# A two-layer sequence block in 32 chunks: the last chunk's mixer products inside the feed-forward part ahead of it, and its result added by VectorE

## The chip, the cores and the metric

The kernel runs on one core of one Trainium2 chip. A core has TensorE (PE) for matrix products, VectorE (DVE), ScalarE (ACT) and GpSimd (POOL) for element-wise work, and SyncE (SP), whose queue issues DMAs. Each runs its instructions in order and they wait for each other by semaphores. The metric is the device time of one execution in microseconds.

## What is computed

Input `x` is 16 x 1024 x 256 (float32). The reference, cut to what matters:

```python
x = x + attn(layernorm(x))     # called the mixer here
x = x + ffn(layernorm(x))

# attn(x)
phi = cumsum((x @ W_omega.T + b_omega) * exp(log_scale) / sqrt(position))
cm_real, cm_imag = x * cos(phi), x * sin(phi)
mem_real = cumsum(cm_real) / position; mem_imag = cumsum(cm_imag) / position
ret_real = mem_real * cos(phi) + mem_imag * sin(phi)
ret_imag = mem_imag * cos(phi) - mem_real * sin(phi)
h = layernorm(concat(cm_real, cm_imag, ret_real, ret_imag)) * gamma + beta
attn = x + gelu(h @ W1.T + b1) @ W2.T + b2      # 1024 -> 512 -> 256

# ffn(x), W1 and W2 rounded to -1, 0, 1
ffn = relu(x @ Wq1.T + b1) @ Wq2.T + b2         # 256 -> 1024 -> 256
```

## The kernel before

The 16384 rows are cut into 32 chunks of 512 (`CHUNKS`, numbered 0 to 31). Float32 operands are split in a high and a low float16 part, so most products come twice or three times. The code of each engine is written out by hand as a loop over steps (`run`, `step`); in step s four to five chunks are in work at once: `now` is chunk s in its feed-forward part, `nxt` (s+1) in the mixer's hidden layer, gelu and output product, `ahead` (s+2) and `far` (s+3) in the phases, scans and first layernorm. The order of the calls in each engine's `step` is the order of its instructions. Near the end of the program `far`, then `ahead`, then `nxt` no longer exist: step 30 has chunk 30 as `now` and chunk 31 as `nxt`, step 31 has chunk 31 alone.

What TensorE does in a step: `hidden(nxt, 0..3)` (L914, 4 x 24 products of 512 columns) with the statistics and `spread` between them; then eight blocks `ffn_in(now, m)` (L929, 4 products of 512 columns each) and `ffn_out(now, m)` (L942, 8 products of 256 columns each), block m out being three blocks (`LAG`) behind block m in; ahead of the last three blocks out comes `mixer_out(nxt, now)` (L959, 48 products of 256 columns).

PSUM, `ps`, has eight banks of 512 float32. Banks 0 and 1 (`ps_rows_a`) take `ffn_out`, banks 4 to 7 `hidden` and then, by turns, the eight blocks of `ffn_in`. `mixer_out` writes banks 4 and 5 (`ps_rows_b`), so it waits until ScalarE has read blocks 4 and 5 of `now` (`relu_done`). Bank 2 holds `spread` (read by ScalarE, L656, `rbs_done`) and bank 3 the sums of the context (read by VectorE, `csq_done`); banks 2 and 3 hold `omega` of `far` where that exists.

Per block of the feed-forward part ScalarE makes `relu` (L694) and its float16 high part `relu_hi` (L703), VectorE the low part `relu_lo` (L1309), in four slots (`SLOTS`); `ffn_out` needs both parts. For the mixer VectorE scales the hidden sums (`scale_hidden`, L1265), ScalarE makes `gelu` (L660) and `gelu_hi` (L666), VectorE `gelu_lo` (L1270).

Behind `mixer_out` a chunk goes through a chain: VectorE adds the residual (`mixer_residual`, L1277, into `x1`), takes the statistics (L1284, L1289, L1295), GpSimd raises to the power -1/2 (L495), VectorE makes the mean term (`lean_2`, L1101), ScalarE normalises (`normalise_2`, L595, four pieces) and makes the high part (`second_hi`, L676), VectorE the low part (`second_lo`, L1301), and SyncE issues four DMA transposes into `turned2` (L440), which `ffn_in` of the chunk reads. These transposes also wait until all blocks `ffn_in` of the chunk before are done (`f1_done`).

The output: GpSimd adds the bias `f_b2` to `x1` by an accumulating DMA (`x1_bias`, L487), SyncE stores `x1` (L452), ScalarE overwrites `x1` with the scaled sums of `ffn_out` (`output`, L608), and GpSimd adds that to what is stored by an accumulating DMA (`output_sum`, L491). GpSimd's queue has, in a step, `inverse_std_2(now)`, `output_sum(before)`, then `x1_bias(now)`.

## Time and profile before

| | |
|---|---|
| median of 3 runs | 1565.07 us (1564.71 to 1565.65) |
| the profiled execution | 1566.02 us |
| its span, first to last instruction | 1564.2 us |
| TensorE busy | 1481.0 us (95%) |
| VectorE, ScalarE, GpSimd busy | 1393.2, 1251.6, 585.8 us |
| mean granted clock of TensorE | 0.985 of full speed |

The span is one execution as the hardware profiler took it; the time of the execution has 1.8 us more around it. TensorE works nearly without a break from about 100 us to 1524 us; a step takes about 43 us in the later part. The page gives busy time as an average over the whole span, so the first and last stages don't show in it, and the timelines of the last 85 us are read for them. A line of a timeline is: start, time, engine, line of the kernel, operation, what it writes and reads, count, and in brackets how long the engine stood before it and who released it.

### The profile page before, as it was taken

The numbers are of one execution on the slowest core, as the hardware profiler recorded it, in microseconds if no ns is written. First come the engines' busy times: TensorE is split into PE (matmuls) and PEld (weight loads), VectorE is DVE, ScalarE is ACT, GpSimd is POOL, SyncE is SP. The second block draws the span as 40 slices with busy tenths as digits, with TensorE's granted clock in tenths as the row PEclk, the third lists the DMA queues.
The fourth block names the chain that finished last, engine by engine and source line by source line (L and its number), as shares of the span: only waits on it lengthen the run. The fifth ranks groups of instructions, "written<-read, shape, count | busy, mean of one in ns | idle before, by whom it ended". The sixth has DMA issues, their size and how long they took to land.

```text
span 1564.2 us, 29917 instructions
## 1 busy us (share of the span) xinstructions
PE 1481.0 (95%) x10677; PEld 875.1 (56%) x10677; DVE 1393.2 (89%) x2322; ACT 1251.6 (80%) x1774; POOL 585.8 (37%) x395
## 2 busy tenths in 40 slices
PE   3789999999999999999999999999999999999994
PEld 2455555665555566555556555555556555655652
DVE  6999999999999999999999999999999999998831
ACT  6768987888888888888878888888788988888743
POOL 1323344443334444333444433344433344433311
PEclk9799999999999999999999999999999999999997
DMA  6325665545665554566555457655555665545424
GB/s 215 70 53 109 122 112 85 107 96 93 118 122 104 93 105 95 95 118 122 99 95 105 95 96 121 122 90 99 101 96 104 122 120 83 105 87 93 82 55 67
DMA packets 234115, 159.25 MB, mean 102 GB/s; under 512 B 140784, under 2 KB 224240, under 8 KB 233968
## 3 DMA queue, kind: packets, MB, share of 16 engines
q0 software_dynamic: 59904, 83.90, 34.9%
q1 hardware_dynamic: 172432, 69.77, 19.2%
q10 hardware_dynamic: 1632, 3.67, 0.6%
q8 instruction: 86, 1.41, 0.4%
q14 instruction: 61, 0.50, 0.1%
HBM read 24.13 MB, written 33.55 MB: 37 GB/s over the span
## 4 chain that ended last, share of the span: by engine, by line
PE 45%; DVE 30%; issue 11%; ACT 6%; SPq 4%; DMA 3%; DVEq 0%; ACTq 0%; POOL 0%; POOLq 0%
PE ps L942 11%; PE ps L959 10%; PE ps L914 10%; PE ps L929 8%; PE ps L874 5%; SPq L440 4%; DVE ph L1152 3%; DVE mi L1184 2%; DMA turned<-rows 2%; DVE mr L1196 2%; DVE bn L1284 2%; DVE mi L1215 2%; DVE xs L1129 2%; DVE rows L1301 2%; DVE arena L1265 2%
## 5 line engine op out<-in xcount | busy, mean ns | idle before, releaser
L914 PE MATMUL ps<-arena,w_hi 128*128 128x512 f16 x2048 | 609.0, 379 | 2.1 <-DVE arena L1241 1.2
L914 PE MATMUL ps<-arena,w_lo 128*128 128x512 f16 x1024 | 388.0, 379 | 0.0
L914 PEld LDWEIGHTS ps<-arena,w_hi 128*128 128x128 f16 x2048 | 197.9, 98 | 223.4 <-issue 2.0
L929 PE MATMUL ps<-turned,fw_t 128*128 128x512 f16 x1024 | 250.1, 382 | 22.6 <-DMA turned<-rows 22.1
L942 PE MATMUL ps<-fw_t,arena 128*128 128x256 f16 x2048 | 254.7, 272 | 9.9 <-DVE arena L1309 9.0
L942 PEld LDWEIGHTS ps<-fw_t,arena 128*128 128x128 f16 x2048 | 193.7, 97 | 92.8 <-issue 39.0
L694 ACT ACTIVATE arena<-ps,relu_bias,relu_scale 128x512 f32<-128x512 f32 x256 | 191.7, 773 | 55.3 <-PE ps L929 55.2
L527 POOL TENSOR_TENSOR sqr<-sqr,turn 128x1024 f32<-128x1024 f32 x32 | 88.8, 2776 | 334.1 <-ACT sqr L642 320.5
L1309 DVE TENSOR_TENSOR arena<-arena 128x512 f16<-128x512 f32 x256 | 170.1, 685 | 28.3 <-ACT arena L703 27.6
L959 PE MATMUL ps<-w_hi,arena 128*128 128x256 f16 x1024 | 173.0, 273 | 0.0
L929 PEld LDWEIGHTS ps<-turned,fw_t 128*128 128x128 f16 x1024 | 98.6, 98 | 124.5 <-DMA turned<-rows 35.8
L914 PEld LDWEIGHTS ps<-arena,w_lo 128*128 128x128 f16 x1024 | 100.1, 98 | 120.8
L703 ACT CAST arena<-arena 128x512 f16<-128x512 f32 x256 | 148.0, 616 | 1.0
L959 PE MATMUL ps<-w_lo,arena 128*128 128x256 f16 x512 | 139.6, 273 | 0.0
L543 POOL TENSOR_TENSOR qa<-mi,sn 128x1024 f32<-128x1024 f32 x32 | 76.6, 2393 | 96.5 <-DVE mr L1196 86.7
L959 PEld LDWEIGHTS ps<-w_hi,arena 128*128 128x128 f16 x1024 | 100.2, 98 | 11.6
L660 ACT ACTIVATE arena<-arena,b_full,z_down 128x512 f32<-128x512 f32 x128 | 100.5, 809 | 1.2 <-DVE arena L1265 0.8
L495 POOL TENSOR_TENSOR rs<-ve,minus_half 128x4 f32<-128x4 f32 x32 | 59.4, 1856 | 97.9 <-DVE ve L1295 97.1
L1270 DVE SCALAR_TENSOR_TENSOR arena<-arena,up 128x512 f16<-128x512 f32 x128 | 94.8, 743 | 0.0
L646 ACT CAST sqr<-sqr 128x512 f16<-128x512 f32 x32 | 19.8, 618 | 91.8 <-POOL sqr L529 91.8
L476 POOL DMA_DIRECT2D rr<-qa x32 | 29.8, 932 | 169.1 <-DVE rr L1231 169.1
L666 ACT ACTIVATE arena<-arena,up 128x512 f16<-128x512 f32 x128 | 90.8, 710 | 0.0
(183 smaller groups left out, 2774.8 us busy)
## 6 DMA issues: line engine op xcount, KB each, us to landing
x_rows<-in_L_attn_x SPq DMA_DIRECT2D x32, 512.0 KB, 4.3
rr<-qa POOLq DMA_DIRECT2D x32, 512.0 KB, 5.0
ri<-qb POOLq DMA_DIRECT2D x32, 512.0 KB, 7.0
base<-bias_rows POOLq DMA_DIRECT2D x32, 512.0 KB, 6.1
x<-bias_rows POOLq DMA_DIRECT2D x32, 512.0 KB, 8.7
out<-x SPq DMA_DIRECT2D x32, 512.0 KB, 5.5
out<-x POOLq DMA_DIRECT2D x32, 512.0 KB, 6.1
arena<-in_L_attn_W ACTq DMA_DIRECT2D x1, 2048.0 KB, 11.3
```

The costliest lines, as they stand in the source:

```text
L527: pool.tensor_tensor(sqr[:, :, :], sqr[:, :, :], turn[:, :, :], ALU.add).then_inc(q2_done, 1)
L660: act.activation(z[:, m], z[:, m], ACT.Gelu, scale=z_down[:, 0:1], bias=b1_full[:, m:m + 1])\
L666: act.activation(gh[:, m], z[:, m], ACT.Copy, scale=up[:, 3:4]).then_inc(gh_done[m], 1)
L694: act.activation(rf[:, m % SLOTS], ps[:, 4 + m % KE], ACT.Relu, scale=relu_scale[:, 0:1], bias=relu_bias[:, m:m + 1]).then_inc(relu_done, 1)
L703: act.copy(rh[:, m % SLOTS], rf[:, m % SLOTS]).then_inc(rh_done, 1)
L874: last = pe.matmul(ps[:, 2 + e], w[:, k, e * P:(e + 1) * P], a[:, k], start=(i == 0), stop=(i == len(passes) - 1))
L914: last = pe.matmul(ps[:, 4 + m], w[:, k, m * P:(m + 1) * P], a[:, c.b, k], start=(i == 0), stop=(i == len(passes) - 1))
L929: last = pe.matmul(ps[:, 4 + m % KE], fw1_t[:, k, m * P:(m + 1) * P], a[:, k], start=(i == 0), stop=(i == len(passes) - 1))
L942: last = pe.matmul(ps_rows_a[:, j], a[:, m % SLOTS, j * P:(j + 1) * P], fw2_t[:, m], start=(m == 0 and j % 2 == 0 and a is rh), stop=(m == ...
L959: last = pe.matmul(ps_rows_b[:, j], a[:, m, j * P:(j + 1) * P], w[:, m], start=(i == 0), stop=(i == len(passes) - 1))
L1270: dve.scalar_tensor_tensor(out=gl[:, m], in0=z[:, m], scalar=up[:, 3:4], in1=gh[:, m], op0=ALU.mult, op1=ALU.subtract).then_inc(gl_done[m], 1)
L1309: dve.tensor_tensor(rl[:, m % SLOTS], rf[:, m % SLOTS], rh[:, m % SLOTS], ALU.subtract)\
```

## The change

It touches steps 30 and 31 of each engine.

- TensorE: `mixer_out` of chunk 31 comes right behind the first four blocks `ffn_in` of chunk 30, ahead of the first block `ffn_out`, and writes banks 2 and 3 (`ps_rows_last`); it waits for `rbs_done` and `csq_done` and no longer for blocks 4 and 5 of relu. The first four blocks `ffn_in` of chunk 31 get a wait for the relu of chunk 30's blocks 4 to 7.
- ScalarE: in step 30 (`last_mixer`) all of chunk 31's gelu comes ahead of chunk 30's relu, each `relu_hi` stands right behind its `relu`, and `normalise_2` and `second_hi` of chunk 31 stand ahead of relu 6. In step 31 `output(30)` is followed by the relus by pairs; the last `output` is gone.
- VectorE: in step 30 `second_lo(30)` comes ahead of `context_variance(31)`, the four `gelu_lo` in a row, and residual and statistics of chunk 31 ahead of relu_lo 3, `lean_2` ahead of relu_lo 5, `second_lo` ahead of relu_lo 6. At the end it has a new `output`, two instructions that add the scaled sums to `x1`.
- SyncE stores chunk 31 in two halves, each behind its add, and not before; GpSimd's last accumulating store is gone.

The order of instructions as built shows it. TensorE, from the first blocks of chunk 30's feed-forward part on, before (`fw_t` with `turned` is ffn_in, `fw_t` with `arena` is ffn_out, `w_hi` and `w_lo` with 128x256 are the mixer's output weights):

```order
L929 MATMUL ps<-turned,fw_t 128x512 x16
L942 MATMUL ps<-fw_t,arena 128x256 x8
L929 MATMUL ps<-turned,fw_t 128x512 x4
L942 MATMUL ps<-fw_t,arena 128x256 x8
...
L942 MATMUL ps<-fw_t,arena 128x256 x8
L959 MATMUL ps<-w_hi,arena 128x256
L959 MATMUL ps<-w_lo,arena 128x256
...
L959 MATMUL ps<-w_hi,arena 128x256
L942 MATMUL ps<-fw_t,arena 128x256 x24
L929 MATMUL ps<-turned,fw_t 128x512 x16
L942 MATMUL ps<-fw_t,arena 128x256 x8
```

and after:

```order
L965 MATMUL ps<-turned,fw_t 128x512 x16
L999 MATMUL ps<-w_hi,arena 128x256
L999 MATMUL ps<-w_lo,arena 128x256
...
L999 MATMUL ps<-w_hi,arena 128x256
L978 MATMUL ps<-fw_t,arena 128x256 x8
L965 MATMUL ps<-turned,fw_t 128x512 x4
L978 MATMUL ps<-fw_t,arena 128x256 x8
L965 MATMUL ps<-turned,fw_t 128x512 x4
...
L978 MATMUL ps<-fw_t,arena 128x256 x32
L965 MATMUL ps<-turned,fw_t 128x512 x16
L978 MATMUL ps<-fw_t,arena 128x256 x8
```

The 48 products stood behind five blocks out and eight in; now they stand behind four blocks in, and all eight blocks out come after them.

ScalarE, from relu 4 of chunk 30 on (L694, L700: relu; L703, L709: relu_hi; `xs`: normalise_2; `rows`: second_hi; `x<-ps`: output), before:

```order
L694 ACTIVATE arena<-ps,relu_bias,relu_scale 128x512 x2
L703 CAST arena<-arena 128x512 x2
L694 ACTIVATE arena<-ps,relu_bias,relu_scale 128x512 x2
L703 CAST arena<-arena 128x512 x2
L608 ACTIVATE x<-ps,down 128x1024
L595 ACTIVATE xs<-x,lean,rs 128x256 x4
L676 CAST rows<-xs 128x4x256
L694 ACTIVATE arena<-ps,relu_bias,relu_scale 128x512
L703 CAST arena<-arena 128x512
```

and after:

```order
L700 ACTIVATE arena<-ps,relu_bias,relu_scale 128x512
L709 CAST arena<-arena 128x512
L700 ACTIVATE arena<-ps,relu_bias,relu_scale 128x512
L709 CAST arena<-arena 128x512
L601 ACTIVATE xs<-x,lean,rs 128x256 x4
L682 CAST rows<-xs 128x4x256
L700 ACTIVATE arena<-ps,relu_bias,relu_scale 128x512
L709 CAST arena<-arena 128x512
L700 ACTIVATE arena<-ps,relu_bias,relu_scale 128x512
L709 CAST arena<-arena 128x512
L614 ACTIVATE x<-ps,down 128x1024
L700 ACTIVATE arena<-ps,relu_bias,relu_scale 128x512
```

Chunk 31's normalisation stood behind all relus of chunk 30 and its output; now it stands between blocks 5 and 6.

VectorE, from the first relu_lo of chunk 30 on (L1309, L1359: relu_lo; L1270: gelu_lo), before:

```order
L1309 TENSOR_TENSOR arena<-arena 128x512 x3
L1270 SCALAR_TENSOR_TENSOR arena<-arena,up 128x512 x2
L1309 TENSOR_TENSOR arena<-arena 128x512
...
L1270 SCALAR_TENSOR_TENSOR arena<-arena,up 128x512
L1309 TENSOR_TENSOR arena<-arena 128x512 x3
L1277 SCALAR_TENSOR_TENSOR x<-ps,h_down,base 128x1024
L1284 BN_STATS bn<-x 128x6 x4
...
L1295 TENSOR_SCALAR ve<-mv 128x4
L1101 SCALAR_TENSOR_TENSOR lean<-rs,mv 128x4
L1301 TENSOR_TENSOR rows<-xs,rows 128x4x256
```

and after:

```order
L1320 SCALAR_TENSOR_TENSOR arena<-arena,up 128x512 x4
L1359 TENSOR_TENSOR arena<-arena 128x512 x3
L1327 SCALAR_TENSOR_TENSOR x<-ps,h_down,base 128x1024
L1334 BN_STATS bn<-x 128x6 x4
...
L1345 TENSOR_SCALAR ve<-mv 128x4
L1359 TENSOR_TENSOR arena<-arena 128x512 x2
L1151 SCALAR_TENSOR_TENSOR lean<-rs,mv 128x4
L1359 TENSOR_TENSOR arena<-arena 128x512
L1351 TENSOR_TENSOR rows<-xs,rows 128x4x256
L1359 TENSOR_TENSOR arena<-arena 128x512 x10
L1367 SCALAR_TENSOR_TENSOR x<-ps,down,x 128x512 x2
```

Residual, statistics and mean term moved ahead of five, then three of the low parts, and two adds stand at the end.

The diff:

```diff
@@ line 203 of before @@
         ps_rows_b = ps[:, 4:6, :].rearrange("p b (t d) -> p (b t) d", d=D)
+        ps_rows_last = ps[:, 2:4, :].rearrange("p b (t d) -> p (b t) d", d=D)
 
@@ line 449 of before @@
                                      rows1[:, j].rearrange("p i d -> p (i d)"), transpose=True).then_inc(turned1_done, 16)
-                if c := s.chunk(0):
+                if (c := s.chunk(0)) and c.index < CHUNKS - 1:
                     need_dma(sp, x1_biased, c)
@@ line 454 of before @@
             run(sp, step, -2)
-            for i in range(2):
-                sp.wait_ge(stored[i], 16 * (CHUNKS // 2))
-                sp.wait_ge(added[i], 16 * (CHUNKS // 2))
+            last = Chunk(Counts(sp, CHUNKS - 2), 1)
+            for half in range(2):
+                need(sp, out_done, last, 0 if half == 0 else -1)
+                sp.dma_start(out_v[last.index][:, 2 * half:2 * half + 2],
+                             x1[:, last.b, 2 * half:2 * half + 2]).then_inc(stored[last.b], 16)
+            sp.wait_ge(stored[0], 16 * (CHUNKS // 2))
+            sp.wait_ge(added[0], 16 * (CHUNKS // 2))
+            sp.wait_ge(stored[1], 16 * (CHUNKS // 2 + 1))
+            sp.wait_ge(added[1], 16 * (CHUNKS // 2 - 1))
 
@@ line 558 of before @@
             run(pool, step, -1)
-            output_sum(Chunk(Counts(pool, CHUNKS - 2), 1))
 
@@ line 704 of before @@
 
+            def last_mixer(before, now, last):
+
+                sums_hi(last)
+                output(before)
+                normalise_2(now)
+                second_hi(now)
+                spread_out(last)
+                for m in range(KE - 1):
+                    gelu(last, m)
+                for m in range(KE - 1):
+                    gelu_hi(last, m)
+                gelu(last, KE - 1)
+                gelu_hi(last, KE - 1)
+                for m in range(KF):
+                    if m == KF - 2:
+                        normalise_2(last)
+                        second_hi(last)
+                    relu(now, m)
+                    relu_hi(now, m)
+
             def step(s):
                 before, now, nxt, ahead, far = s.chunk(-1), s.chunk(0), s.chunk(1), s.chunk(2), s.chunk(3)
+                if now and not ahead:
+                    if nxt:
+                        last_mixer(before, now, nxt)
+                    else:
+                        output(before)
+                        for m in range(KF):
+                            relu(now, m)
+                            relu_hi(now, m)
+                    return
                 if nxt:
@@ line 849 of before @@
             run(act, step, -1)
-            output(Chunk(Counts(act, CHUNKS - 2), 1))
 
@@ line 926 of before @@
                     need(pe, z_done[m], after)
+                else:
+                    need_block(pe, relu_done, m + KE, c, 1)
                 passes = [(a, k) for k in range(KD) for a in (h2, l2)]
@@ line 947 of before @@
             def mixer_out(c, before):
-                if before:
+                if before and c.index < CHUNKS - 1:
                     need_block(pe, relu_done, KE, before)
@@ line 955 of before @@
                     need(pe, gl_done[m], c)
+                if c.index == CHUNKS - 1:
+                    need(pe, rbs_done, c)
+                    need(pe, csq_done, c)
+                rows = ps_rows_last if c.index == CHUNKS - 1 else ps_rows_b
                 for j in range(NT):
@@ line 958 of before @@
                     for i, (a, w, m) in enumerate(passes):
-                        last = pe.matmul(ps_rows_b[:, j], a[:, m, j * P:(j + 1) * P], w[:, m],
+                        last = pe.matmul(rows[:, j], a[:, m, j * P:(j + 1) * P], w[:, m],
                                          start=(i == 0), stop=(i == len(passes) - 1))
@@ line 978 of before @@
                     hidden(nxt, 3)
+                if now and not ahead:
+                    for m in range(KF):
+                        ffn_in(now, m, nxt)
+                        if nxt and m == KE - 1:
+                            mixer_out(nxt, now)
+                        if m >= LAG:
+                            ffn_out(now, m - LAG)
+                    for m in range(KF - LAG, KF):
+                        ffn_out(now, m)
+                    return
                 for m in range(KF):
@@ line 1276 of before @@
                 need_dma(dve, added, c, 2)
-                dve.scalar_tensor_tensor(out=x1[:, c.b], in0=ps_rows_b, scalar=h_down[:, 0:1], in1=base[:, c.b],
-                                         op0=ALU.mult, op1=ALU.add).then_inc(x1_done, 1)
+                dve.scalar_tensor_tensor(out=x1[:, c.b], in0=ps_rows_last if c.index == CHUNKS - 1 else ps_rows_b,
+                                         scalar=h_down[:, 0:1], in1=base[:, c.b], op0=ALU.mult, op1=ALU.add).then_inc(x1_done, 1)
 
@@ line 1311 of before @@
 
+            def output(c):
+                need_block(dve, f2_done, KF - 1, c)
+                need_dma(dve, x1_biased, c)
+                for half in range(2):
+                    to = x1[:, c.b, 2 * half:2 * half + 2]
+                    dve.scalar_tensor_tensor(out=to, in0=ps_rows_a[:, 2 * half:2 * half + 2], scalar=down[:, 4:5],
+                                             in1=to, op0=ALU.mult, op1=ALU.add).then_inc(out_done, 1)
+
+            def last_mixer(now, last):
+
+                lean_2(now)
+                second_lo(now)
+                context_variance(last)
+                for m in range(KE):
+                    scale_hidden(last, m)
+                for m in range(KE):
+                    gelu_lo(last, m)
+                for m in range(KF):
+                    if m == 3:
+                        mixer_residual(last)
+                        statistics_2(last)
+                        spread_2(last)
+                    if m == 5:
+                        lean_2(last)
+                    if m == 6:
+                        second_lo(last)
+                    relu_lo(now, m)
+
             def step(s):
                 now, nxt, ahead, far = s.chunk(0), s.chunk(1), s.chunk(2), s.chunk(3)
+                if now and not ahead:
+                    if nxt:
+                        last_mixer(now, nxt)
+                    else:
+                        for m in range(KF):
+                            relu_lo(now, m)
+                        output(now)
+                    return
                 if now:
```

## Rows read from the trace of the kernel before

**Rows 1.** The page: the span, and three of its groups of instructions (count, busy us, mean ns)

```profile
span 1564.2 us, 29917 instructions
...
L694 ACT ACTIVATE arena<-ps,relu_bias,relu_scale 128x512 f32<-128x512 f32 x256 | 191.7, 773 | 55.3 <-PE ps L929 55.2
...
L1309 DVE TENSOR_TENSOR arena<-arena 128x512 f16<-128x512 f32 x256 | 170.1, 685 | 28.3 <-ACT arena L703 27.6
...
L703 ACT CAST arena<-arena 128x512 f16<-128x512 f32 x256 | 148.0, 616 | 1.0
...
```

**Rows 2.** Busy us (and instructions) by stage, then granted clock, DMA share, GB/s

```profile
...
1524.00:1538.00 14.00, 0.00 (x0) 0.00 (x0) 2.02 (x8) 4.21 (x6) 3.60 (x3) 0.59 0.72 113
1538.00:1544.00 6.00, 5.74 (x15) 2.11 (x16) 0.69 (x1) 2.58 (x4) 0.00 (x0) 0.53 0.25 87
...
1556.00:1564.00 8.00, 0.00 (x0) 0.00 (x0) 0.00 (x0) 0.72 (x1) 1.29 (x1) 0.79 0.51 66
...
```

**Rows 3.** Timeline of TensorE: start us, us, instruction, idle before and releaser

```profile
...
1504.16 3.62 PE L929 MATMUL ps<-turned,fw_t 128*128 128x512 f16 x16
1507.99 1.03 PE L942 MATMUL ps<-fw_t,arena 128*128 128x256 f16 x8 [0.21 <-DVE arena L1309]
...
1515.92 0.27 PE L959 MATMUL ps<-w_hi,arena 128*128 128x256 f16 x1
...
1521.05 0.27 PE L959 MATMUL ps<-w_hi,arena 128*128 128x256 f16 x1
1521.16 2.78 PE L942 MATMUL ps<-fw_t,arena 128*128 128x256 f16 x24
1538.26 6.27 PE L929 MATMUL ps<-turned,fw_t 128*128 128x512 f16 x16 [14.31 <-DMA turned<-rows]
...
1553.67 1.91 PE L942 MATMUL ps<-fw_t,arena 128*128 128x256 f16 x16 [0.45 <-DVE arena L1309]
```

**Rows 4.** Timeline of VectorE, columns as before

```profile
...
1504.36 0.69 DVE L1265 TENSOR_TENSOR arena<-ps,rb 128x512 f32<-128x512 f32 x1 [2.62 <-PE ps L914]
...
1521.36 1.28 DVE L1277 SCALAR_TENSOR_TENSOR x<-ps,h_down,base 128x1024 f32<-128x1024 f32 x1 [3.50 <-PE ps L959]
...
1525.90 0.16 DVE L1101 SCALAR_TENSOR_TENSOR lean<-rs,mv 128x4 f32<-128x4 f32 x1 [1.13 <-POOL rs L495]
1529.36 1.23 DVE L1301 TENSOR_TENSOR rows<-xs,rows 128x1024 f16<-128x1024 f32 x1 [3.30 <-ACT rows L676]
...
```

**Rows 5.** Timeline of ScalarE

```profile
...
1526.18 2.07 ACT L595 ACTIVATE xs<-x,lean,rs 128x256 f32<-128x256 f32 x4 [1.08 <-DVE lean L1101]
...
1555.61 1.11 ACT L608 ACTIVATE x<-ps,down 128x1024 f32<-128x1024 f32 x1 [2.30 <-PE ps L942]
```

**Rows 6.** Timeline of SyncE's queue

```profile
...
1495.52 5.12 SPq L440 DMA_TRANSPOSE turned<-rows  x4
...
1530.67 6.32 SPq L440 DMA_TRANSPOSE turned<-rows  x4
...
```

**Rows 7.** Timeline of GpSimd

```profile
...
1557.02 1.29 POOL L491 DMA_DIRECT2D out<-x  x1 [27.17 <-ACT x L608]
```

**Rows 8.** DMA issues, 1494 to 1510 us, then 1556 on: KB, us to landing

```profile
...
out<-x SPq DMA_DIRECT2D x1, 512.0 KB, 3.1
turned<-rows SPq DMA_TRANSPOSE x4, 2.5
...
out<-x POOLq DMA_DIRECT2D x1, 512.0 KB, 6.1
```

**Rows 9.** Stages as in rows 2, short ones in which the granted clock changed

```profile
...
92.00:94.00 2.00, 0.00 (x0) 0.00 (x0) 2.00 (x3) 1.97 (x4) 0.00 (x0) 0.74 0.44 90
1526.50:1527.00 0.50, 0.00 (x0) 0.00 (x0) 0.00 (x0) 0.50 (x2) 0.50 (x1) 0.58 0.00 0
1543.50:1544.00 0.50, 0.50 (x4) 0.17 (x3) 0.00 (x0) 0.40 (x1) 0.00 (x0) 0.86 0.00 0
...
```

**Rows 10.** Timeline of TensorE, early in the program

```profile
...
94.04 0.26 PE L1023 MATMUL ps<-rows,x 128*128 128x128 f16 x1 [3.10 <-ACT fw_t L784]
...
```

## The prediction

> **What bounds the kernel now.** I read the page first, then the busy time by stage, then the timeline of each engine behind 1500 us. The span is 1564.2 us [rows 1] and the profiled execution took 1566.02 us; the three timed runs have their median at 1565.07 us. So 1.8 us lie outside the span, and the profiled execution is 0.95 us above the median. The diff leaves all of the program up to chunk 29's feed-forward part as it was, so the sum is made over the last 85 us of the span and the difference is taken off both numbers.
>
> In that tail TensorE sets the pace up to 1523.9 us and then the kernel is a chain of latencies. TensorE does nothing between 1524 and 1538 us [rows 2]: its timeline shows chunk 30's feed-forward products, then chunk 31's mixer products (L959, 1515.92 to 1521.32), 24 products left over from chunk 30, and 14.31 us of waiting for the DMA transposes of chunk 31 [rows 3]. What it waits for can be followed step by step. VectorE adds the residual at 1521.36, takes the statistics, GpSimd the power, VectorE has the mean term at 1525.90 [rows 4], ScalarE normalises at 1526.18 [rows 5], VectorE's low part runs 1529.36 to 1530.59 [rows 4], SyncE issues four transposes from 1530.67 on [rows 6], and the products start at 1538.26. Behind the last product (1555.58) come ScalarE's copy at 1555.61 [rows 5], GpSimd's accumulating store at 1557.02 [rows 7], and the end at 1564.2. Nothing else is running in either wait, so a microsecond taken out of these two chains is a microsecond of the kernel.
>
> **The mixer products of chunk 31 come 8 us earlier.** TensorE's order of instructions in chunk 30's part becomes: four blocks in (L929's 16 products), mixer_out of chunk 31 (48 products), and then the eight blocks out and four blocks in by turns. The products are the same in number; they write banks 2 and 3 in place of 4 and 5. Those are free once ScalarE has copied the spread and VectorE has read the sums, long before, so the two added waits (rbs_done, csq_done) cost nothing. When can they start? TensorE has the 16 products done at 1504.16 + 16 x 0.216 = 1507.6. Every low part of the gelu must be there: VectorE's fourth scale_hidden starts at 1504.36 and takes 0.69 [rows 4]; in the new order ScalarE does gelu 3 and gelu_hi 3 right behind it, ahead of all of relu, and VectorE has four gelu_lo in a row. By 0.77 + 0.62 us on ScalarE and about 0.7 us on VectorE (L694, L703 and L1309 are of the same size of tile) [rows 1] that is 1505.05 + 0.77 + 0.62 + 0.69 = 1507.2 for the fourth low part behind its high part, or, counted along VectorE's four in a row, 1505.05 + 4 x 0.69 = 1507.8. Before, TensorE also stood 0.21 us here for the first relu_lo, until 1507.99 [rows 3]. So I put the mixer products at 1507.95, their end at 1507.95 + 5.40 = 1513.35 and the residual at 1513.4 instead of 1521.36.
>
> From there the chain is the same as before, with two things in its way. VectorE has relu_lo 3 and 4 between the statistics and the mean term: the power is there at 1513.4 + 4.5 = 1517.9, and the two pieces, 0.65 us each, run from 1516.8 to 1518.1, so 0.2 us is lost. ScalarE has relu 5 and its high part ahead of the normalisation; block 5 is in at 1513.2 + 4 x 0.87 = 1516.7, and 0.77 + 0.62 us later it is 1518.1, so nothing is lost. The normalisation thus starts at 1518.4, not 1526.18: **7.8 us earlier**. Behind it ScalarE's order holds relu 6 and 7 back until 1521.4 and TensorE stands some 2 us in chunk 30's last three blocks and ends them near 1525.9 instead of 1523.9. That is off the path: the transposes need only all eight blocks in (1520.1), and chunk 30's result is out of the banks (ScalarE, 1.1 us) by 1527.0, before chunk 31 needs them. POOL's bias for chunk 31 now stands behind the accumulating store of chunk 30 and so goes out at 1528, 0.3 us earlier than before at best; it is needed only near 1543.
>
> **The transposes.** SyncE took 6.32 us to issue the four of chunk 31 and 5.12 for those of chunk 30 [rows 6], and the last lands 2.5 us behind its issue [rows 8]. In the slow case GpSimd's store of chunk 30 and its bias for chunk 31 were moving in the same 4 us. Now the transposes go out from 1522.9 to 1528.0 and that store, which waits for 1527, can have no byte moving before that, when the last of the four (1526.8) is already out. I take 5.12, **1.2 us less**. Issue of the fourth at 1522.9 + 3.85, landing 2.5, and TensorE starts at 1529.25: 9.0 us earlier than 1538.26. Its wait shrinks from 14.3 to some 3.35 us.
>
> **The clock.** Before, the granted clock fell to its lower level (1.2 of 2.4 GHz) at 1526.6, 2.7 us behind the last product, and came back at 1543.6, 5.4 us after the products had begun again [rows 9]; half of these 5.4 us, 2.7, is lost. A wait of 3.10 us early in the trace [rows 10] also had a fall in it, 2.0 us behind the last product [rows 9]. So a wait of 3.35 us with some 2 us of standing just ahead of it very probably has one too, and what is saved is small. The loss has 0 (no fall) and about 3 us as its ends; I take 2.2, a little under the 2.7 of the nearest row because the engine has been idle for less, so **0.5 us less**. The Trainium skill's page "TensorE: Matmul & The Clock Gate" (Part 1 and the section on oscillation behind it) says that the throttled state is the default and that activity releases it, and names waits for DMA in a loop as what throttles it again; this trace agrees, with the falls at 1526.6 us and before 94 us, both in idle stretches [rows 9]. By that rule alone the shortening of the wait would return nothing at all here, and the forecast would be 0.5 us higher.
>
> **The last feed-forward part.** 32 products in and 64 out take the same 13.9 us at the full clock. ScalarE now has each high part right behind its relu, so the stand of 0.45 us before the last 16 products [rows 3] goes: 1.39 us per block of ScalarE [rows 1] against 1.73 us of TensorE keeps up. **0.5 us less.**
>
> **The last result.** Before: from the last product at 1555.58 to 1564.2, 8.6 us: copy 1.1, GpSimd's issue at 1557.02, landing 6.1 us later [rows 7, 8], 1.1 us of closing. Now: VectorE adds two halves straight from the banks. One half has the size of a scale_hidden (0.69), the whole that of the residual (1.28) [rows 4], so both are done at +1.35; SyncE issues each half behind it, and the plain store of a whole chunk landed 3.1 us after its issue in a quiet stretch [rows 8]. A half has half the bytes: between 1.55 and 3.1, I take 2.5, since part of 3.1 is not data. 0.05 + 1.35 + 0.1 + 2.5 + 1.1 = 5.1, so **3.5 us less**. The bias of chunk 31 has landed long before and costs nothing; if it had not, this add is what would wait. "DMA: Bandwidth & Descriptors" of the Trainium skill (the sections Specifications and Latency and other measured facts) gives 0.6 us against 1 us as the latency to the first byte of a store from SyncE and from GpSimd. By that alone the path would save 0.4 us on the queue; the rows show 3.1 against 6.1 us for the same 512 KB, and the rows decide.
>
> **Sum.** 7.8 + 1.2 + 0.5 + 0.5 + 3.5 = 13.5 us. 1564.2 becomes 1550.7 in the span, the profiled execution 1552.5, and the median 1565.07 - 13.5 = 1551.6 us, 0.9% less.
>
> **Rivals.**
> (a) The clock does not fall in the shorter wait. For it: it fell 2.0 and 2.7 us behind a last product, so its moment is not fixed. Against: both are under 3.35. It would give 2.2 us more, 1549.4.
> (b) The store or the transposes are slow: the transposes again take 6.32 us, or ScalarE's and VectorE's new interleaving holds the normalisation back by a relu pair (1.4 us), or the halves need 3.1 us each to land. Each is 0.6 to 1.4 us and they can add up: 1553 to 1554.5.
> (c) The change does not do what it says, the mixer products find gelu_lo late and TensorE stands with chunk 30's blocks queued behind them. Each microsecond of that is one on the path. With the mixer products starting where they did, at 1515.92 [rows 3], only the tail's 3.5 and 0.5 would be left: 1561. Against it: the order shows gelu 3 and its parts ahead of the relus.
> (d) Slower than before: the stand of 0.3 us ahead of the mixer products and the later ones let the clock fall within chunk 30 and it stays low. Then 5.4 us of mixer products take 5.4 more and the last part 13.9 - 2.2 more: 13.5 is outweighed by 17.1, 1568.7. It decides from 13.5 us of extra work at the lower level on the path. Against it: the stand of 0.21 us at 1507.99 left the clock at its full level, and it came back in 5.4 us the one time it was low here.
>
> **How the numbers follow.** Forecast 0.72, (a) 0.10, (b) 0.14, (c) 0.02, (d) 0.01, and 0.01 for a gain within the bound. The forecast's own ends are the loss to the clock at 1.2 to 2.9 us and the landing at 1.6 to 3.1: 1549.7 to 1552.9. The range takes in (a) and (b): 1548.9 to 1554.4. A measurement of this kernel can tell 0.2%, 3.1 us, from no change. All of the forecast, (a), (b) and (c) is faster by more than that: 0.98; same 0.01, slower 0.01.
>
> **What would show it.** TensorE's timeline: mixer products from 1508, first products of chunk 31 at 1529.2, a wait of 3 to 3.5 us before them, with the clock falling in or just ahead of it. SyncE: transposes from 1522.9, 5.1 us long. VectorE: residual at 1513.4 and the normalisation on ScalarE at 1518.4. At the end two adds of 0.7 us and the end of the span some 5.1 us after the last product. I am wrong if the residual starts after 1515, if TensorE's stand inside chunk 30 reaches the eight blocks in (then the transposes wait for them), or if the stores land after more than 3.1 us.

## The result, and the profile after

| | before | after |
|---|---|---|
| median | 1565.14 us (6 runs, 1562.27 to 1565.88) | 1551.21 us (6 runs, 1549.32 to 1552.36) |
| profiled execution, its span | 1566.02, 1564.2 us | 1552.36, 1550.6 us |
| mean granted clock | 0.985 | 0.990 |

The ratio is 0.9912, with a 95% interval of 0.9899 to 0.9925: 13.9 us less. The forecast was 1551.6.

TensorE's timeline of the changed kernel answers to [rows 3] (L965 is ffn_in, L978 ffn_out, L999 mixer_out):

```profile
1504.34 3.62 PE L965 MATMUL ps<-turned,fw_t 128*128 128x512 f16 x16
1508.24 0.27 PE L999 MATMUL ps<-w_hi,arena 128*128 128x256 f16 x1 [0.28 <-issue]
...
1513.48 1.04 PE L978 MATMUL ps<-fw_t,arena 128*128 128x256 f16 x8
...
1524.23 1.03 PE L978 MATMUL ps<-fw_t,arena 128*128 128x256 f16 x8 [1.90 <-DVE arena L1359]
1525.56 1.03 PE L978 MATMUL ps<-fw_t,arena 128*128 128x256 f16 x8 [0.30 <-DVE arena L1359]
1530.54 5.31 PE L965 MATMUL ps<-turned,fw_t 128*128 128x512 f16 x16 [3.95 <-DMA turned<-rows]
...
1542.64 3.66 PE L978 MATMUL ps<-fw_t,arena 128*128 128x256 f16 x32
```

The 48 mixer products start at 1508.24 behind a stand of 0.28 us and end when block 0 out begins, 1513.5; before it was 1515.92 to 1521.3. The wait before the last part is 3.95 us and not 14.31, and the last 32 products run without a stand. VectorE's rows, to be held against [rows 4], and GpSimd's power:

```profile
1513.68 1.28 DVE L1327 SCALAR_TENSOR_TENSOR x<-ps,h_down,base 128x1024 f32<-128x1024 f32 x1 [2.14 <-PE ps L999]
...
1518.60 0.16 DVE L1151 SCALAR_TENSOR_TENSOR lean<-rs,mv 128x4 f32<-128x4 f32 x1 [0.30 <-POOL rs L502]
...
1522.06 1.23 DVE L1351 TENSOR_TENSOR rows<-xs,rows 128x1024 f16<-128x1024 f32 x1 [2.70 <-ACT rows L682]
...
1546.33 1.41 DVE L1367 SCALAR_TENSOR_TENSOR x<-ps,down,x 128x512 f32<-128x512 f32 x2 [1.34 <-PE ps L978]
```

```profile
1517.17 1.39 POOL L502 TENSOR_TENSOR rs<-ve,minus_half 128x4 f32<-128x4 f32 x1 [21.56 <-DVE ve L1345]
```

ScalarE's normalisation ([rows 5] has it at 1526.18) and SyncE's queue ([rows 6]); in the last row the two stores of the halves:

```profile
1518.88 2.08 ACT L601 ACTIVATE xs<-x,lean,rs 128x256 f32<-128x256 f32 x4 [0.30 <-DVE lean L1151]
```

```profile
1488.71 7.34 SPq L441 DMA_TRANSPOSE turned<-rows  x4
...
1523.37 5.74 SPq L441 DMA_TRANSPOSE turned<-rows  x4
1547.11 1.03 SPq L459 DMA_DIRECT2D out<-x  x2
```

DMA issues of the changed kernel, first in the stretch of the transposes (1523 to 1531 us), then behind 1538 us, to be held against [rows 8]. In the upper part stand also the queues (packets and MB behind the title, share of the 16 engines):

```profile
DMA packets 2212, 0.58 MB, mean 73 GB/s; under 512 B 2176, under 2 KB 2210, under 8 KB 2210
...
q14 instruction: 1, 0.01, 1.1%
q8 instruction: 1, 0.02, 0.8%
...
out<-x POOLq DMA_DIRECT2D x1, 512.0 KB, 6.4
...
turned<-rows SPq DMA_TRANSPOSE x4, 2.9
```

```profile
out<-x SPq DMA_DIRECT2D x2, 256.0 KB, 2.2
```

The spans differ by 1564.2 - 1550.6 = 13.6 us. To see where they went I count from TensorE's first product of chunk 30's part, because the program's way up to there isn't equally long in two executions (below). It starts at 1504.16 before and 1504.34 after; from there to the end it is 60.0 us before and 46.3 after:

| piece | before | after | difference | forecast |
|---|---|---|---|---|
| chunk 30's part begins, to the first transpose's issue | 26.51 | 19.03 | 7.5 | 7.8 |
| first transpose's issue, to the last part's first product | 7.59 | 7.17 | 0.4 | 1.2 |
| last part: lost to the lower clock | 2.7 | 1.7 | 1.0 | 0.5 |
| last part: the rest | 14.6 | 14.05 | 0.6 | 0.5 |
| last product, to the end of the span | 8.63 | 4.31 | 4.3 | 3.5 |

The sum was right to 0.3 us, but two of its terms were off by 0.8: what the transposes did not give, the clock and the last store did. That the errors cancel is luck, and the closeness of the sum says less than the terms do. Differences here and below are taken before rounding. The experiments below take the terms one by one.

### The profile page after: what moved, and what is told of

The parts are those of the page before. It is cut to its first block, busy times and chain, and to the rows that moved or that the text cites. A ratio compares the mean times of both kernels' runs of the same rounds, so it can differ in the third digit from the quotient of the medians.

```text
span 1550.6 us, 29919 instructions
## 1 busy us (share of the span) xinstructions
PE 1480.5 (95%) x10677; PEld 875.2 (56%) x10677; DVE 1395.3 (90%) x2324; ACT 1252.0 (81%) x1773; POOL 583.3 (38%) x394
## 3 DMA queue, kind: packets, MB, share of 16 engines
q8 instruction: 86, 1.41, 0.4%
## 4 chain that ended last, share of the span: by engine, by line
PE 47%; DVE 30%; issue 9%; ACT 5%; SPq 4%; DMA 4%; DVEq 0%; ACTq 0%; POOL 0%; POOLq 0%
PE ps L978 11%; PE ps L948 11%; PE ps L999 10%; PE ps L965 8%; PE ps L908 5%; SPq L441 4%; DVE ph L1202 3%; DVE mi L1234 3%; DMA turned<-rows 2%; DVE mr L1246 2%; DVE bn L1334 2%; DVE xs L1179 2%; DVE mi L1265 2%; DVE rows L1351 2%; DVE arena L1315 2%
## 5 line engine op out<-in xcount | busy, mean ns | idle before, releaser
L978 PE MATMUL ps<-fw_t,arena 128*128 128x256 f16 x2048 | 254.6, 272 | 11.9 <-DVE arena L1359 10.9
L965 PE MATMUL ps<-turned,fw_t 128*128 128x512 f16 x1024 | 249.1, 381 | 11.5 <-DMA turned<-rows 11.1
L978 PEld LDWEIGHTS ps<-fw_t,arena 128*128 128x128 f16 x2048 | 193.7, 97 | 94.0 <-issue 39.3
L700 ACT ACTIVATE arena<-ps,relu_bias,relu_scale 128x512 f32<-128x512 f32 x256 | 191.8, 773 | 49.0 <-PE ps L965 49.0
L1359 DVE TENSOR_TENSOR arena<-arena 128x512 f16<-128x512 f32 x256 | 170.6, 686 | 20.6 <-ACT arena L709 19.8
L999 PE MATMUL ps<-w_hi,arena 128*128 128x256 f16 x1024 | 173.2, 273 | 0.3 <-issue 0.3
L965 PEld LDWEIGHTS ps<-turned,fw_t 128*128 128x128 f16 x1024 | 98.3, 98 | 112.7 <-DMA turned<-rows 25.0
L709 ACT CAST arena<-arena 128x512 f16<-128x512 f32 x256 | 148.6, 616 | 1.5
L999 PE MATMUL ps<-w_lo,arena 128*128 128x256 f16 x512 | 139.7, 273 | 0.0
L999 PEld LDWEIGHTS ps<-w_hi,arena 128*128 128x128 f16 x1024 | 100.3, 98 | 12.4 <-issue 0.7
L1315 DVE TENSOR_TENSOR arena<-ps,rb 128x512 f32<-128x512 f32 x128 | 82.1, 683 | 10.9 <-ACT rb L662 6.5
```

Source lines behind the costliest of these rows:

```text
L700: act.activation(rf[:, m % SLOTS], ps[:, 4 + m % KE], ACT.Relu, scale=relu_scale[:, 0:1], bias=relu_bias[:, m:m + 1]).then_inc(relu_done, 1)
L709: act.copy(rh[:, m % SLOTS], rf[:, m % SLOTS]).then_inc(rh_done, 1)
L965: last = pe.matmul(ps[:, 4 + m % KE], fw1_t[:, k, m * P:(m + 1) * P], a[:, k], start=(i == 0), stop=(i == len(passes) - 1))
L978: last = pe.matmul(ps_rows_a[:, j], a[:, m % SLOTS, j * P:(j + 1) * P], fw2_t[:, m], start=(m == 0 and j % 2 == 0 and a is rh), stop=(m == ...
L999: last = pe.matmul(rows[:, j], a[:, m, j * P:(j + 1) * P], w[:, m], start=(i == 0), stop=(i == len(passes) - 1))
L1315: dve.tensor_tensor(z[:, m], ps[:, 4 + m], rb[:, :], ALU.mult).then_inc(z_done[m], 1)
```

## How the runs are compared

The table gives, for the one profiled execution of each kernel, the pieces that the timelines show, in us. "To first product" is from the issue of the first transpose of chunk 31 to TensorE's first product with it; in e3 part of it is TensorE itself, which was still busy with added products. "Clock" is half of the time in the last part at the lower level. "From chunk 30" is from chunk 30's first product in to the end of the span. Median and ratio are those of the runs of that label.

| kernel | chunk 30 begins | to first product | last part | clock | last product to end | from chunk 30 | median | ratio (95%) |
|---|---|---|---|---|---|---|---|---|
| before | 1504.16 | 7.59 | 17.32 | 2.7 | 8.63 | 60.0 | 1565.14 | |
| changed | 1504.34 | 7.17 | 15.75 | 1.7 | 4.31 | 46.3 | 1551.21 | 0.9912 (0.9899 to 0.9925) |
| e1 | 1504.03 | 7.44 | 16.52 | 2.5 | 8.39 | 51.4 | 1556.78 | 0.9957 (0.9942 to 0.9972) |
| e2 | 1500.19 | 7.57 | 17.18 | 2.6 | 4.25 | 55.5 | 1558.13 | 0.9964 (0.9950 to 0.9977) |
| e3 | 1503.31 | 7.98 | 14.06 | 0 | 4.24 | 45.3 | 1550.33 | 0.9913 (0.9900 to 0.9927) |
| e4 | 1502.64 | 7.66 | 15.75 | 1.7 | 4.83 | 47.3 | 1551.66 | 0.9920 (0.9908 to 0.9933) |
| e5 | 1500.86 | 9.13 | 16.97 | 3.0 | 4.27 | 54.5 | 1556.45 | 0.9954 (0.9941 to 0.9967) |
| e6 | 1503.90 | 7.25 | 16.67 | 2.7 | 4.25 | 47.2 | 1553.59 | 0.9935 (0.9920 to 0.9950) |
| e7 | 1500.58 | 9.46 | 16.72 | 2.1 | 4.22 | 49.4 | 1551.69 | 0.9927 (0.9914 to 0.9940) |
| e8 | 1503.34 | 8.04 | 14.07 | 0 | 4.23 | 45.4 | 1549.66 | 0.9915 (0.9898 to 0.9931) |
| e9 | 1502.15 | 6.88 | 16.70 | 2.7 | 4.24 | 46.9 | 1550.49 | 0.9920 (0.9905 to 0.9935) |
| e10 | 1501.92 | 6.38 | 15.73 | 1.7 | 4.24 | 45.4 | 1550.47 | 0.9926 (0.9909 to 0.9942) |
| e11 | 1501.40 | 6.38 | 15.75 | 1.7 | 4.29 | 45.6 | 1549.31 | 0.9914 (0.9900 to 0.9929) |
| e12 | 1502.97 | 6.39 | 14.07 | 0 | 4.25 | 43.7 | 1548.58 | 0.9912 (0.9898 to 0.9925) |

The second column is the warning in this table: up to there TensorE has the same work (e9 to e12 have 64 products of one column more at the head), and it takes from 1500.2 to 1504.3 us. So a median carries some 2 us that have nothing to do with the edit, and the kernel before itself had medians of 1564.32, 1563.50, 1562.48 and 1563.23 us beside the experiments. Effects of 1 us are read from the column "from chunk 30" and from the rows.

## Experiments: the two halves of the change

**e1: the last result as before.** On the changed kernel:

```diff
 # SyncE: stores chunk 31 before the sum again, in one piece; its two stores at the end go
-                if (c := s.chunk(0)) and c.index < CHUNKS - 1:
+                if c := s.chunk(0):
 # GpSimd, ScalarE: behind the last step
+            output_sum(Chunk(Counts(pool, CHUNKS - 2), 1))
+            output(Chunk(Counts(act, CHUNKS - 2), 1))
 # VectorE, last step
-                        output(now)
```

> The changed kernel with the last result made as before the change: ScalarE scales it, GpSimd adds it to what SyncE has stored. Theory (two chains, each worth its own length): the last result is worth 4.3 us, so 1551.2 + 4.3 = 1555.5 us, and in the trace the last part's first product starts near 1530.5 as in the changed kernel. Rival (the gain comes mostly from the store, the earlier products are given back to the clock and to slower transposes): 1559 us or more.

Measured: 1556.78 us. From chunk 30 to the end it is 51.4 us: 8.7 less than before and 5.1 more than the changed kernel. Of these 5.1, 8.39 - 4.31 = 4.1 are the last result, 0.3 the transposes and 0.8 the clock, which in this execution fell at 1525.26, before TensorE's wait had begun, and came back at 1535.50. A stage of it:

```profile
1525.00:1526.00 1.00, 0.76 (x4) 0.58 (x5) 0.09 (x1) 0.00 (x0) 0.00 (x0) 0.63 0.46 91
```

The forecast was 1555.5 and the median is 1.3 above it, 2.2 below the 1559 of the rival. The traces are clearer: most of the gain of the earlier products stays.

**e2: the last result alone.** On the kernel before:

```diff
-            output(Chunk(Counts(act, CHUNKS - 2), 1))
-            output_sum(Chunk(Counts(pool, CHUNKS - 2), 1))
 # VectorE behind the last step: the two adds; SyncE: the two stores
+            output(Chunk(Counts(dve, CHUNKS - 2), 1))
```

> The kernel before with only the last result changed: VectorE adds it in two halves and SyncE stores each. Theory: 1565.1 - 4.3 = 1560.8 us, from the last product to the end 4.3 us, and the wait before the last part's products 14.3 us as before. Rival (the two parts need each other): the sum of this gain and of that of the mixer alone is not the 13.9 us of both, by more than 1.5 us.

Measured: 1558.13 us, 6.2 less than the kernel before beside it and not 4.3. Its end is as forecast. Timeline of the end, VectorE's two adds and SyncE's two stores:

```profile
1551.49 1.41 DVE L1321 SCALAR_TENSOR_TENSOR x<-ps,down,x 128x512 f32<-128x512 f32 x2 [1.49 <-PE ps L946]
1552.27 1.03 SPq L458 DMA_DIRECT2D out<-x  x2
```

From the last product to the end it is 4.25 us for 8.63. From chunk 30 on it gains 60.0 - 55.5 = 4.5; the rest of the 6.2 lies ahead of chunk 30, where the code is the same and the profiled execution was 4 us ahead of that of before. By the medians the two halves give 7.5 and 6.2, together 13.7 for the 13.9 of both; by the traces 8.7 and 4.5, together 13.2 for 13.8. They add up.

**e5: the mixer products five blocks later.**

```diff
-                        if nxt and m == KE - 1:
-                            mixer_out(nxt, now)
                         if m >= LAG:
                             ffn_out(now, m - LAG)
+                        if nxt and m == KE + 1:
+                            mixer_out(nxt, now)
```

> The changed kernel with chunk 31's mixer products five blocks of TensorE later (behind block 5 in and block 2 out of chunk 30, not behind block 3 in). Five blocks are 5 x 0.87 = 4.35 us, and block 0 out then waits for the first relu_lo, about 1509, which adds 0.5. Theory (from the mixer products to the last part every microsecond is on the path): 1551.2 + 4.9 = 1556.1 us, give or take 0.6 for the clock. Rival (the transposes wait for something else, such as the eight blocks in or ScalarE's relus): less than 2 us more, 1553 at most.

Measured: 1556.45 us for 1556.1. The products start 9.02 us behind chunk 30's first and not 3.90, and the first transpose is issued 24.16 us behind it and not 19.03: 5.12 us later at the one end, 5.13 at the other. So every microsecond of their place is on the path to the transposes, as the prediction held. Behind that this kernel lost 2 us more in the transposes and 1.3 in the clock (table), so from chunk 30 on it is 8.2 us longer than the changed kernel, where the forecast was 4.9. That the median came out at the forecast all the same is luck: the profiled execution reached chunk 30 3.5 us earlier than that of the changed kernel.

## Experiments: the last result and the last part's order

**e4: one add and one store.**

```diff
-                for half in range(2):
-                    to = x1[:, c.b, 2 * half:2 * half + 2]
-                    dve.scalar_tensor_tensor(out=to, in0=ps_rows_a[:, 2 * half:2 * half + 2], ...)
+                dve.scalar_tensor_tensor(out=x1[:, c.b], in0=ps_rows_a, ...)
```

> The changed kernel with the last result added in one instruction and stored in one DMA. Theory (a half is in flight while the other is made, and a half lands 2.2 us behind its issue and the whole 3.1): 0.1 us less on VectorE, 0.9 us more to landing, so 0.6 to 0.8 us more, 1551.9 us, and 5.1 us from the last product to the end. Rival (both halves share the same DMA engines, so splitting gains nothing): 1551.2 us or 0.2 less, 4.3 us.

The end of it, and how long the store took to land:

```profile
1545.11 1.28 DVE L1363 SCALAR_TENSOR_TENSOR x<-ps,down,x 128x1024 f32<-128x1024 f32 x1 [1.34 <-PE ps L976]
1546.42 0.38 SPq L458 DMA_DIRECT2D out<-x  x1
```

```profile
out<-x SPq DMA_DIRECT2D x1, 512.0 KB, 2.9
```

From the last product to the end it is 4.83 us for 4.31 (forecast 5.1). The add is 0.13 shorter (1.28 for 1.41), the landing 0.7 longer (2.9 for 2.2). So the halves are worth 0.5 us; the median, 0.45 above, can't show that by itself, but the eleven traces with halves have 4.22 to 4.31 us in this column of the table. The Trainium skill ("DMA: Bandwidth & Descriptors", Rules for kernel authors) advises against splitting one transfer over two partition halves, since both use the same engines. Here each half takes all 128 partitions and half of what a partition holds, and the first is issued while the second is still being added; so split, the store paid.

**e7: the old order of ScalarE in the last part.**

```diff
-                        for m in range(KF):
-                            relu(now, m)
-                            relu_hi(now, m)
+                        relu(now, 0)
+                        relu_hi(now, 0)
+                        relu(now, 1)
+                        relu(now, 2)
+                        relu_hi(now, 1)
+                        relu_hi(now, 2)
+                        ...
```

> The changed kernel with ScalarE's order in the last part as before the change (relu 1 and 2, then their high parts, and so on, instead of each high part behind its relu). Theory: TensorE stands 0.45 to 0.6 us before the last 16 products as it did before, 1551.8 us. Rival (the stand came from the low clock at the start of that part and not from the order): no stand, 1551.2 us.

TensorE's timeline of this kernel; the number in brackets is the stand:

```profile
1529.06 5.67 PE L978 MATMUL ps<-turned,fw_t 128*128 128x512 f16 x16 [6.24 <-DMA turned<-rows]
...
1543.87 1.91 PE L991 MATMUL ps<-fw_t,arena 128*128 128x256 f16 x16 [0.45 <-DVE arena L1372]
```

The 0.45 us before the last 16 products are there again, as in [rows 3], and are not there in the changed kernel (L978 at 1542.64 above, 32 products in one row). The last part is 16.72 us. Less 2.1 for the clock that is 14.6, as in the kernel before (17.32 - 2.7), where the changed kernel has 14.05. The order was the cause.

## Experiments: the clock

Stages of the changed kernel in which the granted clock changed, columns as in [rows 2]:

```profile
1531.00:1531.50 0.50, 0.50 (x3) 0.23 (x2) 0.00 (x0) 0.00 (x0) 0.00 (x0) 0.63 1.05 125
1534.50:1535.00 0.50, 0.50 (x3) 0.20 (x2) 0.00 (x0) 0.50 (x1) 0.00 (x0) 0.95 1.27 205
```

It fell at 1531.1, when the last part's products had already begun, and was back at 1534.5. So 3.4 us ran at 1.2 GHz, and half of it is lost.

**e3: products that nobody reads in the wait.**

```diff
+            def keep_busy(c, count):
+                need(pe, x1_done, c)
+                for i in range(count):
+                    pe.matmul(ps[:, 2], w1_hi[:, i % KC, 0:P], ch[:, c.b, i % KC], start=True, stop=True)
                     for m in range(KF - LAG, KF):
                         ffn_out(now, m)
+                    if nxt:
+                        keep_busy(nxt, 15)
```

> The changed kernel with 15 products of 512 columns that nobody reads behind chunk 30's last block out (3.2 us at the full clock), in the wait for the transposes. Theory (the wait lets the clock fall and that costs 1.7 us in the last part): the granted clock stays at its upper level up to the end, the first 16 products of the last part are 3.6 us long and not 5.3, 1549.5 us. Rival (the clock is not what paces the last part, or falls anyway): 1551.2 us. If the added products were late for the last part's own they would cost up to 0.5 us and the trace would show no wait before these.

Stages of this kernel, then TensorE's timeline:

```profile
1524.00:1525.00 1.00, 0.70 (x7) 0.40 (x5) 0.37 (x1) 0.00 (x0) 0.00 (x0) 0.85 0.31 63
1525.00:1528.00 3.00, 3.00 (x11) 1.50 (x10) 0.00 (x0) 1.11 (x1) 0.12 (x1) 0.50 0.47 86
```

```profile
1523.19 1.03 PE L978 MATMUL ps<-fw_t,arena 128*128 128x256 f16 x8 [1.89 <-DVE arena L1366]
1524.52 1.73 PE L978 MATMUL ps<-fw_t,arena 128*128 128x256 f16 x8 [0.30 <-DVE arena L1366]
```

The last part is 14.06 us, 1.7 less than 15.75, so that the clock's price in it is shown to be what half the time at the lower level says. But the expectation that the clock would stay up was wrong: it was at 0.50 from 1525 to 1528. It fell at 1524.7, behind the stand of 1.89 us before block 6 out, not in the wait. With the added products it was back at 1528.1; in e1, e6 and e9, where it fell at the same place (21.0 to 21.4 us behind chunk 30's first product) and no products were added, it stayed low until the last part had run for 5.0 to 5.4 us. As the added products ran in part at the lower clock they ended late (1530.26), and the last part began right behind them, 0.05 us, while the last packet of the transposes had ended at 1529.16. So TensorE's own added work held the last part back, as the expectation had allowed for, and from chunk 30 on only 1.0 us of the 1.7 was gained.

**e8: 6 more ahead of block 6 out.**

```diff
                     for m in range(KF - LAG, KF):
+                        if nxt and m == KF - 2:
+                            keep_busy(nxt, 6)
                         ffn_out(now, m)
```

> As the variant with 15 added products, and 6 more ahead of block 6 out of chunk 30, where TensorE stood 1.9 us. Theory (that stand together with the wait can already bring the clock down in some executions): 1549.4 us as with 15 alone, with the mean granted clock of every run alike and the spread of the times smaller. Rival (6 added products hold up blocks 6 and 7): these end 1.3 us later, off the path, no change to the variant with 15 alone unless the last part waits for chunk 30's output.

In the trace the clock did not fall before the last product had ended (1547.27 us), and the last part is 14.07 us. The median is 1549.66; its six runs spread over 1546.75 to 1555.28, more than any other's, so the forecast of a smaller spread did not hold. Nor was the mean clock alike: five runs had 0.991 or 0.992 and one 0.988. The run of 1555.28 had 0.992, so the clock did not make its time; what did is open. From chunk 30 on it is 45.4 us, no better than e3: TensorE was free 1.58 us before the last part, but the transposes took 8.04 us. That led to the last question.

## Experiments: why the transposes took 7 to 9 us

The prediction gave 6.35 (3.85 to the fourth issue and 2.5 to its landing) and the changed kernel took 7.17. The other variants with the early mixer products had 7.3 to 9.5 up to here.

**e6: GpSimd's transfers held back.**

```diff
                 if before:
+                    if not nxt:
+                        need_turned(pool, now)
                     output_sum(before)
```

> The changed kernel with GpSimd's store of chunk 30 and bias of chunk 31 held until the transposes of chunk 31 have landed. In the changed kernel these took 5.74 us to issue, the fourth 1.89 against 1.27, and landed 3.3 us behind its issue against 2.5 of the quiet ones. Theory (the fetch of instructions that the DMA view shows in that stretch holds one DMA engine up, not GpSimd's traffic): no change, 1551.2, and the transposes again near 5.7 us if such a fetch falls into them and 5.1 if not. Rival (GpSimd's issue and traffic slow the fourth one): transposes 5.1 us, the last part 0.8 us earlier, 1550.4 us.

GpSimd's store was issued at 1530.61, behind the last transpose's landing, and still the transposes took 5.99 us to issue and 7.25 to the first product:

```profile
1530.61 1.35 POOL L498 DMA_DIRECT2D out<-x  x1 [12.49 <-DMA turned<-rows]
```

```profile
DMA packets 2178, 0.55 MB, mean 65 GB/s; under 512 B 2176, under 2 KB 2176, under 8 KB 2176
...
q1 hardware_dynamic: 2176, 0.52, 32.8%
q8 instruction: 1, 0.02, 0.7%
q14 instruction: 1, 0.01, 0.3%
...
turned<-rows SPq DMA_TRANSPOSE x4, 3.3
```

For the changed kernel the rival is out; in its own trace, too, GpSimd's first packet starts at 1530.14, 6.8 us behind the first issue, when the transposes' last packet (1529.94) has ended. The median was 1553.59, 2.4 above the changed kernel's and above the forecast; from chunk 30 on it is 0.9 more, all of it clock (2.7 for 1.7), and the rest is not explained. What is left beside the transposes are two packets of instruction fetch, of 16 KB on q8 and 8 KB on q14. The same two stand in the changed kernel's answer above, and in the traces of all variants with the early products up to here. In the kernel before, the q8 packet next to this place was fetched at 1522.7, while TensorE still worked at chunk 30's last blocks and the transposes were 8 us off. In both kernels TensorE had at that point passed the same number of its instructions, within 10. The single packet took 1.07 us in the changed kernel (q8, 1526.98) and 1.42 (q14, 1527.74), where one of the transposes' own 2048 packets of 256 bytes takes 0.02. In the changed kernel four of these, all of the third transpose, took 0.9 to 1.1 us, and the data of the third and with it of the fourth came late. How a fetch does that is not shown: the record doesn't say which of the 16 DMA engines a packet used.

In two variants GpSimd had a part after all. In e5 and e7 the data of the transposes ended 7.0 us behind the first issue, just when GpSimd's packets began to move, and the last of the transposes' closing packets of 4 bytes ended at 8.8 and 9.1 us; in e10 it ended 0.2 us behind the data. DMA answer of e7 from 1526.6 to 1529.0 us:

```profile
DMA packets 312, 0.29 MB, mean 120 GB/s; under 512 B 32, under 2 KB 312, under 8 KB 312
...
q0 software_dynamic: 280, 0.29, 111.8%
q1 hardware_dynamic: 32, 0.00, 2.0%
```

So some 2 us of the 9.13 and 9.46 in the table go with GpSimd's traffic, into which the late transposes ran; no run separates the two there.

**e9, e10, e11: the code shifted against its fetches.** The work of all engines in the tail is left as it is.

```diff
 # e9, e10, e11: head of TensorE's program
+            for i in range(64):
+                pe.matmul(ps[:, 3, 0:1], ones_h[:, :], ones_h[:, 0:1], start=True, stop=True)
 # e10: head of ScalarE's
+            for i in range(64):
+                act.wait_ge(p_ones, 1)
 # e11: head of VectorE's
+            for i in range(64):
+                dve.wait_ge(p_ones, 1)
```

> The changed kernel with 64 products of one column that nobody reads at the head of TensorE's program, where it waits for data. They shift TensorE's code against the 16 KB pieces in which queue q8 fetches it. In all traces with the early mixer products one such piece is fetched at the end of chunk 30's part, while the transposes run, and from the first transpose's issue to the last part's first product it was 7.2 to 9.5 us; the one quiet case (chunk 30's transposes in the kernel before) would give 6.35. Theory (the fetches hold single DMA engines up, and the transposes with them): no q8 packet within the transposes, 6.4 to 7.2 us, the last part some 0.5 to 1.5 us earlier against the start of chunk 30's part. Rival (the transposes are slow for another reason and the fetches only stand beside them): 7.2 us or more with no q8 packet there.

> As the variant with 64 added products, and 64 waits that are already met at the head of ScalarE's program, which shift its code too. Theory: if the 8 KB piece that queue q14 fetches within the transposes is ScalarE's, it goes elsewhere and the stretch from first issue to first product is 6.4 us; if it is another engine's it stays, and the stretch is as in the variant without these waits.

> As the variant with 64 added products, and 64 waits that are already met at the head of VectorE's program. Theory: if the 8 KB piece within the transposes is VectorE's, it goes elsewhere and the stretch is 6.4 us; if not, it stays. Both this and the variant with ScalarE's waits leave all work as it is, so their times differ from the changed kernel by at most 1.5 us for the transposes, plus what the clock does by chance.

The DMA answers in the stretch of the transposes of e9 and of e10:

```profile
DMA packets 2177, 0.53 MB, mean 74 GB/s; under 512 B 2176, under 2 KB 2176, under 8 KB 2176
...
q14 instruction: 1, 0.01, 0.5%
...
turned<-rows SPq DMA_TRANSPOSE x4, 2.5
```

```profile
DMA packets 2472, 0.83 MB, mean 79 GB/s; under 512 B 2176, under 2 KB 2472, under 8 KB 2472
...
q1 hardware_dynamic: 2176, 0.52, 24.9%
q0 software_dynamic: 296, 0.30, 24.5%
...
turned<-rows SPq DMA_TRANSPOSE x4, 2.5
```

SyncE's queue and TensorE's first products in e10:

```profile
1520.95 5.12 SPq L441 DMA_TRANSPOSE turned<-rows  x4
```

```profile
1527.33 1.89 PE L967 MATMUL ps<-turned,fw_t 128*128 128x512 f16 x4 [3.16 <-DMA turned<-rows]
```

With q8 out of the stretch it is 6.88 us, with q14 out too (e10) 6.38, in each case with 5.12 us for the four issues; that is the 6.35 of the quiet case. In e10 none of the 256-byte packets took over 0.05 us. In e9 the q14 packet began at 1526.26, 5.1 us behind the first issue, as the fourth transpose's data began, and took 0.63 us. In e11 it is still there too, at 1524.93, but 4.4 us behind the first issue, at the end of the third one's data; it took 0.45 us and cost nothing: 6.38 as well. So the time of the transposes is shown to hang on where the fetches fall.

The q14 packet is ScalarE's. It starts in the changed kernel and in e11 alike just as ScalarE ends chunk 30's `output` (1526.63 + 1.11 = 1527.74 in the changed kernel), and in e10 it is gone from there and stands at 1507.52. VectorE's shift moved another one: in e11 a q14 packet is at 1514.76, and the one that the other kernels have near the end (1543.69 in the changed kernel) is gone.

**e12: both finds together**, with 6 + 12 added products and the shift of e10.

```diff
+                        if nxt and m == KF - 2:
+                            keep_busy(nxt, 6)
                         ffn_out(now, m)
+                    if nxt:
+                        keep_busy(nxt, 12)
```

> The changed kernel with the two finds together: the shift of TensorE's and ScalarE's code (64 added products and 64 met waits at the head) and 6 + 12 added products of 512 columns in TensorE's two stands at the end of chunk 30. Theory: the transposes take 6.4 us from first issue to first product and the clock stays at its upper level, so from the start of chunk 30's part to the end it is 45.4 (the shifted variant) less its 1.7 us of clock, 43.7 us against 46.3 in the changed kernel, and the last part 14.0 us long; the median 2 to 2.5 us below the changed kernel's, 1549. Rival (the gains of clock and transposes do not add up, since the added products are late for the earlier last part): 44.5 us or more, and no wait before the last part.

```profile
1520.80 1.46 PE L1008 MATMUL ps<-arena,w_hi 128*128 128x512 f16 x6
1522.86 1.03 PE L980 MATMUL ps<-fw_t,arena 128*128 128x256 f16 x8 [0.60 <-DVE arena L1372]
...
1525.05 2.75 PE L1008 MATMUL ps<-arena,w_hi 128*128 128x512 f16 x12
1528.38 3.63 PE L967 MATMUL ps<-turned,fw_t 128*128 128x512 f16 x16 [0.58 <-DMA turned<-rows]
...
1538.79 3.66 PE L980 MATMUL ps<-fw_t,arena 128*128 128x256 f16 x32
```

From chunk 30 to the end it is 43.7 us, as forecast, 2.5 less than the changed kernel: 6.39 for the transposes, 14.07 for the last part, at the full clock throughout. The median, 1548.58 us, is 2.6 below the changed kernel's 1551.21, but its ratio to the kernel before, 0.9912 (0.9898 to 0.9925), is no better than the changed kernel's own, since the kernel before was faster beside it (1563.23). So 2.5 us of the tail are shown by the trace, and a faster kernel as a whole is not shown.

## Why the prediction was right, step by step

- **The mixer products earlier: 7.8, measured 7.5.** The start was put 3.8 us behind chunk 30's first product and is 3.9. (Of the prediction's two counts for the fourth low part of the gelu, the first adds up to 1507.1 and not 1507.2; the later one, 1507.8, decided, and VectorE's four were done at 1507.9.) The 0.3 us come from GpSimd's power: VectorE has the mean term 4.9 us behind the residual (1513.68 to 1518.60) and not 4.5, and stood 0.30 us for it; the power took 1.39 us where the one before took 1.01. The two relu_lo ahead of it, which the prediction charged with 0.2 us, ended before it and cost nothing. relu 5 did not hold the normalisation back. e5 shows that all of this place is on the path.
- **TensorE's later stand in chunk 30.** Put at some 2 us and off the path; it was 1.90 and 0.30. Off the path it was for the transposes, but not for the clock: in e1, e3, e6 and e9 the fall came behind it.
- **The transposes: 1.2, measured 0.4.** This is the term that was mis-sized most for its size. The step was that without GpSimd's transfers, which were moving in the kernel before, the transposes would be as quick as the quiet ones. The new slowness has another source: issued 7.5 us sooner, they now have a fetch of TensorE's code among them that in the kernel before had been done 8 us ahead of them. Rival (b), 6.32 us to issue again, was met to about half (5.74), and not by the cause that the prediction had looked at; in e5 and e7 the late transposes ran into GpSimd's transfers on top of it.
- **The clock: 0.5, measured 1.0.** The fall was foreseen. Its price depends on the execution: 1.7 in the changed kernel's trace and in e4, e10 and e11, 2.1 to 3.0 in the other variants with the early products and no added ones. In e6 and e9 it was 2.7, as in the kernel before, so there nothing was gained. Rival (a), no fall, was met in none of these.
- **The order of the relus: 0.5, measured 0.6;** e7 gives it back.
- **The last result: 3.5, measured 4.3.** A half landed in 2.2 us and not 2.5, and from landing to the end of the span it was 0.6 us and not 1.1: the second issue at 1547.8 landed at 1550.0 of 1550.6. e2 has the same 4.25 us on the kernel before.
- Rivals (c) and (d) did not come: the stand before the mixer products is 0.28 us, and the clock was up through chunk 30 in the changed kernel's trace. In e1, e3, e6 and e9 it did fall within chunk 30's last products, behind the stand of 1.9 us, but the mixer products were long done and it came back.
